# Perceiver layer on one core: last but one cross chunk written out, closing steps moved forward, weight slots exchanged

## What is computed

```python
x = x + cross_attention(layernorm(x), ctx, key_bias, key_mask)   # 16 heads of 32
x = x + self_attention(layernorm(x))     # q, k, v, scores, probabilities, output clamped to [1e-7, 1 - 1e-7]
x = x + experts(layernorm(x))            # 8 experts, each takes its top 32 rows of 128 of every batch:
                                         # gelu(xin @ w1[e]) @ w2[e], 512 -> 2048 -> 512, scattered back
```

## Time and profile before

| | |
|---|---|
| median of 3 runs | 496.81 us (496.67 to 500.01) |
| the profiled execution | 499.95 us, of it span 498.2 us |
| PE busy | 439.1 us (88%) |
| DVE busy | 377.1 us (76%) |
| ACT busy | 288.4 us (58%) |
| POOL busy | 85.6 us (17%) |
| mean granted clock of PE | 0.955 |

### The profile page before, as it was taken

The page is one execution under the profiler, slowest core; times in us unless marked ns, Lnnn a source line. Parts: engine busy times, 40 slices in busy tenths (PEclk is TensorE's granted clock), DMA queues, the critical chain, the costliest instruction groups (busy, mean ns, idle before and its releaser), DMA issues. The chain is left out here.

```text
span 498.2 us, 9477 instructions
## 1 busy us (share of the span) xinstructions
PE 439.1 (88%) x3262; PEld 361.4 (73%) x3262; DVE 377.1 (76%) x495; ACT 288.4 (58%) x594; POOL 85.6 (17%) x87
## 2 busy tenths in 40 slices
PE   0798999999996489997897399999999999999993
PEld 0687888888885377886775378787878787878782
DVE  4679766777777857655697779989898989898963
ACT  0445666666664331356514068787878787878752
POOL 4000000000003201000004214040404040404000
PEclk9999999999999589998998599999999999999998
DMA  6980000000000192231000019999998989898102
GB/s 222 319 313 22 23 23 21 21 21 21 21 21 0 35 349 81 86 108 62 3 2 0 1 52 391 387 387 387 378 374 308 369 305 359 309 369 302 42 0 84
DMA packets 42908, 81.95 MB, mean 164 GB/s; under 512 B 2952, under 2 KB 3080, under 8 KB 42888
## 3 DMA queue, kind: packets, MB, share of 16 engines
q1 hardware_dynamic: 39576, 76.16, 42.8%
q10 hardware_dynamic: 3312, 5.52, 3.2%
HBM read 80.58 MB, written 1.10 MB: 164 GB/s over the span
## 5 line engine op out<-in xcount | busy, mean ns | idle before, releaser
L1010 DVE TENSOR_TENSOR w_lo<-att_w,w_hi 128x2048 fp32r<-128x2048 f32 x60 | 137.8, 2306 | 22.7 <-ACT w_hi L573 22.7
L573 ACT CAST w_hi<-att_w 128x2048 fp32r<-128x2048 f32 x60 | 115.1, 1918 | 15.4 <-PE po L1345 15.4
L422 ACT ACTIVATE big_a<-ps,negm 128x128 f32<-128x128 f32 x176 | 62.2, 402 | 30.1 <-DVE negm L746 30.1
L1345 PE MATMUL po<-w_hi,ht_hi 128*128 128x512 f32 x128 | 51.9, 406 | 0.0
L1345 PE MATMUL po<-w_hi,ht_lo 128*128 128x512 f32 x128 | 50.6, 395 | 0.0
L1345 PE MATMUL po<-w_lo,ht_hi 128*128 128x512 f32 x128 | 50.6, 395 | 0.0
L1055 PE MATMUL pk<-ctx_s,att_w 128*128 128x128 f32 x352 | 42.2, 279 | 0.6 <-DMA ctx_s<-in_ctx_t 0.6
L422 ACT ACTIVATION_READ_ACCUMULATOR big_a<-ps,negm 128x1 f32 x176 | 42.7, 243 | 0.0
L1055 PEld LDWEIGHTS pk<-ctx_s,att_w 128*128 128x128 f32 x352 | 40.1, 192 | 2.9 <-issue 1.8
L743 DVE TENSOR_REDUCE mc<-ps 128x8 f32<-128x1024 f32 x22 | 26.8, 1220 | 13.2 <-PE ps L1122 13.2
L1345 PEld LDWEIGHTS po<-w_hi,ht_lo 128*128 128x128 f32 x128 | 24.1, 188 | 5.7
(11 more groups left out here) (274 smaller groups left out, 980.1 us busy)
## 6 DMA issues: line engine op xcount, KB each, us to landing
att_w<-in_w SPq DMA_DIRECT2D x64, 1024.0 KB, 6.8
ctx_s<-in_ctx_t SPq DMA_DIRECT2D x11, 256.0 KB, 2.5
x_s<-in_x SPq DMA_DIRECT2D x1, 1024.0 KB, 5.8
att_w<-in_wk SPq DMA_DIRECT2D x1, 1024.0 KB, 8.3
att_w<-in_wq SPq DMA_DIRECT2D x1, 1024.0 KB, 10.7
att_w<-in_wv SPq DMA_DIRECT2D x1, 1024.0 KB, 6.9
att_w<-in_wo ACTq DMA_DIRECT2D x1, 1024.0 KB, 6.6
att_w<-in_sq ACTq DMA_DIRECT2D x1, 1024.0 KB, 10.2
```

The costliest lines, as they stand in the source:

```text
L422: ins = a.activation(big_a[:, h], ps[:, c, g * P:(g + 1) * P], ACT.Exp, bias=negm[:, h:h + 1], accum_out=sums[:, h:h + 1])
L573: a.copy(w_hi[:, i % SLOTS], att_w[:, i]).then_inc(hi_ok, 1)
L1010: v.tensor_tensor(w_lo[:, i % SLOTS], att_w[:, i], w_hi[:, i % SLOTS], ALU.subtract).then_inc(lo_ok, 1)
L1345: ins = mm(dst, l, r, start=start and i == 0, stop=i == len(terms) - 1, skip_group_check=True)
```

## The change

The loops over chunks end one earlier, at `prev` = `last` - 1, read from a further entry of `table`, and chunk `prev` is written out with some steps added (`at_end`): DVE forms `reciprocals(0, 2)`, `attended(0)` and `attended(1)` between its copies, PE turns batch 0 between the transposes of the probabilities and the last quarter of the values projection, and ACT and DVE split it. In the last softmax PE issues the out-projections of batches 0 and 1 ahead of and between the transposes of the probabilities; batch 2 is closed between DVE's copies, batch 3 at the end. `maxima` is cut into two halves, and the values' evacuation of the last chunk stands between them. The order of the self attention's turned batches and value projections is changed: `cross_project(3)` ahead of `values_project(0)`, and each `values_project(b)` directly behind `turn_batch(2, b)`. The value weights now go to slot 3 in the prologue; the query weights go to slot 1, split by ACT and DVE in the last softmax and behind it. POOL's two split operations and its `zero` tensor are gone. The self attention's output weights go to slot 1 instead of 3, and the first expert's slots are split in the order 2, 0, 3, 1, with the waits (2, 4, 4, 4).

```diff
-        ot_s = att_w[:, 4, 0].rearrange("p (k t) -> p k t", k=KC)
+        ot_s = att_w[:, 6, 0].rearrange("p (k t) -> p k t", k=KC)
...
-        SPLITS = ((wq_s, 2, in_wq), (wv_s, 1, in_wv), (sq_s, 3, in_sq), (wo_s, 2, in_wo), (sv_s, 1, in_sv), (sk_s, 0, in_sk), (so_s, 3, in_so))
-        TURN_BANKS = [[0, 1, 2, 3], [4, 5, 6, 7], [0, 1, 2, 6], [4] * 4, [4] * 4]
+        SPLITS = ((wq_s, 2, in_wq), (wv_s, 1, in_wv), (sv_s, 3, in_sv), (wo_s, 2, in_wo), (sq_s, 1, in_sq), (sk_s, 0, in_sk), (so_s, 1, in_so))
+        TURN_BANKS = [[0, 1, 2, 3], [4, 4, 0, 7], [5, 4, 1, 2], [4] * 4, [4] * 4]
         V2_BANKS = [3, 0, 1, 4]
-        CROSS_BANKS = [4, 5, 4, 5]
+        CROSS_BANKS = [5, 4, 1, 2]
...
# SP: loads of the first expert's tiles
                 if i == 4:
-                    sp.wait_ge(bt_mm, last + 1)
+                    sp.wait_ge(att_lo_ok, 5)
                 if i == 5:
                     sp.wait_ge(att_lo_ok, 6)
                 if i == 6:
+                    sp.wait_ge(bt_mm, last + 1)
+                if i == 7:
                     sp.wait_ge(att_lo_ok, 7)
...
# POOL
-            g.tensor_tensor(w_hi[:, 1], sv_s, zero[:].unsqueeze(2).broadcast_to([P, KC, D]), ALU.add).then_inc(att_hi_ok, 1)
-            pool.wait_ge(att_hi_ok, 5)
-            g.tensor_tensor(w_lo[:, 1], sv_s, w_hi[:, 1], ALU.subtract).then_inc(att_lo_ok, 1)
...
# ACT
-            with act.Fori(1, last) as t:
+            with act.Fori(1, prev) as t:
                 split_chunk(t + 1)
                 softmax_chunk(t, True)
+            split_chunk(last)
+            softmax_chunk(prev, True)
+            transposed(1, 0)
+            turned_out(last)
             exponents(last, 0)
+            transposed(1, 1)
             exponents(last, 1)
-            turned_out(last)
             rescaling(last)
-            for b in range(B - 1):
-                transposed(1, b)
             exponents(last, 2)
             exponents(last, 3)
+            split_att(4)
             turned_last(last)
+            transposed(1, 2)
             turned_out(last + 1)
-            transposed(2, 0)
             transposed(1, 3)
-            for b in range(1, B):
+            for b in range(B):
                 transposed(2, b)
-            act.wait_ge(att_lo_ok, 5)
             split_att(5)
...
# DVE, end of chunk(t, before, at_end)
                 rescale(t, running(state, t))
-                for c in range(3):
-                    turned_probs(t, c)
+                turned_probs(t, 0)
+                if at_end:
+                    dve.wait_ge(total_ok, t)
+                    dve.wait_ge(summed, t)
+                    reciprocals(0, 2)
+                turned_probs(t, 1)
+                if at_end:
+                    attended(0)
+                turned_probs(t, 2)
                 add_sums(t)
+                if at_end:
+                    attended(1)
+                    transposed(1, 0)
...
# DVE, the last chunk, as it stands after the change
            maximum(last, nm, 0)
            dve.wait_ge(pv_mm, last)
            v_evacuate(last)
            maximum(last, nm, 1)
            moved_maxima(last, nm)
            transposed(1, 1)
            turned_probs(last, 0)
            add_values(prev, last)
            turned_probs(last, 1)
            dve.wait_ge(total_ok, last)
            dve.wait_ge(summed, last)
            reciprocals(2, 3)
            attended(2)
            turned_probs(last, 2)
            rescale(last, running(state, last))
            add_sums(last)
            cross_output(0)
            transposed(1, 2)
            add_values(last, last + 1)
            dve.wait_ge(total_ok, last + 1)
            dve.wait_ge(summed, last + 1)
            reciprocals(3, 4)
            attended(3)
            normed_batch(2, 0)
            transposed(1, 3)
            cross_output(1)
            transposed(2, 0)
            normed_batch(2, 1)
            cross_output(2)
            normed_batch(2, 2)
            transposed(2, 1)
            split_att(4)
            cross_output(3)
            transposed(2, 2)
            normed_batch(2, 3)
...
# PE, chunk(t, before, at_end)
                 turn_probs(t, 3)
+                if at_end:
+                    pe.wait_ge(k_out, t + 2)
+                    turn_batch(1, 0)
                 v_project(t + 1, 3)
                 scores(t + 1)
                 values(t)
...
# PE, behind the loop, as it stands after the change
            chunk(prev, True, at_end=True)
            pe.wait_ge(tr_lo_ok[1], 1)
            turn_batch(1, 1)
            turn_values(last)
            pe.wait_ge(v_out, last + 1)
            pe.wait_ge(att_lo_ok, 4)
            cross_project(0)
            turn_probs(last, 0)
            turn_probs(last, 1)
            cross_project(1)
            turn_probs(last, 2)
            turn_probs(last, 3)
            pe.wait_ge(pt_dve, last * 3 + 1)
            turn_batch(1, 2)
            values(last)
            turn_values(last + 1)
            cross_project(2)
            turn_batch(1, 3)
            turn_batch(2, 0)
            cross_project(3)
            values_project(0)
            turn_batch(2, 1)
            values_project(1)
            turn_batch(2, 2)
            values_project(2)
            turn_batch(2, 3)
            pe.wait_ge(tr_lo_ok[2], B)
            pe.wait_ge(att_lo_ok, 5)
            project_t(1, banks[4:8], q2_mm)
...
-                pe.wait_ge(lo_ok, (2, 3, 3, 4)[q] if isinstance(e, int) and e == 0 else e * 8 + (q + 1))
+                pe.wait_ge(lo_ok, (2, 4, 4, 4)[q] if isinstance(e, int) and e == 0 else e * 8 + (q + 1))
```

More of the change, by code:

```diff
@@ L670, in _ @@
             v.tensor_copy(table[:, 0:n_at], pv[0:1, 0:n_at]).then_inc(table_ok, 1)
-            v.tensor_scalar(table[:, n_at:n_at + 1], pv[0:1, n_at:n_at + 1], -1.0, None, ALU.add).then_inc(table_ok, 1)
+            for i in range(2):
+                v.tensor_scalar(table[:, n_at + i:n_at + i + 1], pv[0:1, n_at:n_at + 1], -1.0 - i, None, ALU.add).then_inc(table_ok, 1)
             statistics(3)
@@ L780, in add_sums, with reciprocals, attended, chunk @@
                 v.tensor_tensor(row, row, sums[:], ALU.add).then_inc(total_ok, 1)
-            def chunk(t, before):
+            def reciprocals(first, end):
+                now = slice(first, end)
+                link(v.tensor_scalar(norm_c[:, now], neg_max[:, now], 0.1 * MASKED, None, ALU.is_lt))
+                link(v.tensor_tensor(total[:, now], norm_c[:, now], total[:, now], ALU.mult))
+                link(v.reciprocal(total[:, now], total[:, now]))
+                link(v.tensor_tensor(norm_c[:, now], norm_c[:, now], total[:, now], ALU.mult))
+            def attended(b):
+                v.tensor_tensor(natural(norm[:, b]), natural(state[:, b]), by_head(norm_c[:, b]), ALU.mult).then_inc(normed[1], 1)
+            def chunk(t, before, at_end=False):
                 nm = running(neg_max, t)
-                maxima(t, nm)
+                maximum(t, nm, 0)
+                maximum(t, nm, 1)
                 if before is not None:
@@ L793, in chunk @@
                 rescale(t, running(state, t))
[L794 to L795 removed]
+                turned_probs(t, 0)
[7 more added lines that the diff above has]
+                turned_probs(t, 2)
                 add_sums(t)
+                if at_end:
+                    attended(1)
+                    transposed(1, 0)
             chunk(0, None)
[L799 removed]
+            with dve.Fori(1, prev) as t:
                 chunk(t, t - 1)
[L802 to L811 removed]
+            chunk(prev, prev - 1, at_end=True)
             def cross_output(b):
@@ L821, in _ @@
             nm = running(neg_max, last)
-            maxima(last, nm)
+            maximum(last, nm, 0)
+            dve.wait_ge(pv_mm, last)
+            v_evacuate(last)
+            maximum(last, nm, 1)
             moved_maxima(last, nm)
-            add_values(last - 1, last)
+            transposed(1, 1)
+            turned_probs(last, 0)
+            add_values(prev, last)
+            turned_probs(last, 1)
             dve.wait_ge(total_ok, last)
             dve.wait_ge(summed, last)
-            reciprocals(0, B - 1)
-            for b in range(B - 1):
-                attended(b)
-            dve.wait_ge(pv_mm, last)
-            v_evacuate(last)
-            transposed(1, 0)
-            transposed(1, 1)
-            transposed(1, 2)
-            rescale(last, running(state, last))
-            turned_probs(last, 0)
-            turned_probs(last, 1)
-            cross_output(0)
-            turned_probs(last, 2)
-            normed_batch(2, 0)
-            cross_output(1)
-            add_sums(last)
+            reciprocals(2, 3)
+            attended(2)
+            turned_probs(last, 2)
+            rescale(last, running(state, last))
+            add_sums(last)
+            cross_output(0)
+            transposed(1, 2)
             add_values(last, last + 1)
@@ L845, in _ @@
             dve.wait_ge(summed, last + 1)
-            reciprocals(B - 1, B)
```

(6 more changed lines are left out.)

85 lines of the change are left out of this document (36 added, 49 removed).

## The result

| | median, us | runs | ratio to before |
|---|---|---|---|
| before | 498.14 (496.51 to 500.01) | 13 | |
| after | 495.03 (493.81 to 496.86) | 13 | 0.9934 [0.9919, 0.9949] |

The kernel is 3.1 us faster, where 5.9 was forecast. Its time of 495.03 us lies inside the stated range (487.5 to 495.5), near its upper end, and 4.1 above the forecast of 490.9. The profiled execution of after took 494.46 us for a span of 492.8; that of before took 499.95 for 498.2, so this pair of traces differs by 5.4 and the medians by 3.1.

A forecast was written before the change was run, and what follows sets the result against it. PE bounds the experts; ahead of them, `negm` held beside POOL's operations delays the last softmax. Query projection 7.6 us earlier, less 1.7 in the first expert, gives 5.9: 496.81 to 490.9 us, range 487.5 to 495.5.

The forecast's parts named there:

- The removed stalls: Last softmax: both `negm` fall from 2.45 and 3.31 us to 0.15; `values(last)` some 10.5 behind `values(prev)`, instead of 26.2.
- the stall at `turn_batch(1, 0)`: Written-out chunk: PE stalls 1.0 us for `attended(0)`, plus 0.4 for the turn; `values(prev)` 1.5 us later.
- the three rounds: Before the query projection: three times turn, 2.0 us round with nothing beside it, then product; PE idles 1.6 each.
- the new wait in the first expert: `hidden(0, 1)` waits for slot 1's split, the fourth: PE stands 1.7 us, paid in full.
- ACT's split: Last softmax: ACT's `split_att(4)`, 1.92 us, beside PE's second out-projection costs nothing; uncovered, up to 1.9.
- D: Rival: engines run dry of instructions in the written-out chunk, up to 3.31 us a stall, 504.1 with four; chance 0.06.
- C: Rival: longer rounds, from `table` reads showing in full or an uncovered split, about +2.7 us, 493.6; chance 0.12.
- A: Rival: clock falls at 168 to 172 us, or before's median runs lose nothing at 172.64: +2.0, 492.9; chance 0.20.
- the last widening: Range 488.4 to 494.6 extended by 0.9 on either side, because the runs of before spread over 3.3 us.
- B: Rival: the low-clock stretch behind 230 us may not come once moved by 7.6 us: 2.0 gained, 488.9; chance 0.12.
- the 2.0 for the clock in Part 2: Last softmax: 2.0 us gained because the first out-projection, 4.90 us at half clock, would run at full clock.
- Part 5: Prologue: one more small DVE instruction and `table` read, and an exchanged load order, cost 0 (bound 0.5 for the reads).

The follow-up runs named there:

- e5: Before with chunk `prev` written out behind the loop, no step moved, slots and POOL's operations kept: 498.49 us, ratio 1.0005.
- e8: The kernel before run once more without an edit, for a second profile: 497.44 us, span 495.7.
- e1: The kernel after run once more without an edit: 495.58 us, ratio to before 0.9938.
- e12: The kernel after, unedited, in one job with its partner that keeps the tile `zero`: 495.03 us, ratio to before 0.9908.
- e9: After with the unused 4-byte tile `zero` allocated again: 492.99 us, ratio to before 0.9903.
- e13: After with the tile `zero` kept, in one job with unedited after: 494.02 us, ratio to before 0.9894.
- e4: After with each `values_project(b)` one turn later and DVE's `split_att(4)` behind the last normalisation: 490.54 us, ratio to before 0.9837.
- e3: After with the self attention's output weights in slot 2, so `hidden(0, 1)` waits for the second split: 493.54 us, ratio to before 0.9893.
- e6: After with PE's `turn_batch(1, 0)` behind the last quarter of `v_project` in the written-out chunk: 494.38 us, ratio to before 0.9919.
- e10: After with the edits of e3, e4 and e6 together and the tile `zero` kept: 487.45 us, ratio to before 0.9791.

## Why the prediction was right and wrong

**The mechanism of every part was right.** The removed stalls, the stall at `turn_batch(1, 0)`, the three rounds and the new wait in the first expert stand in the trace where they were put, with 1.7 for 1.5, 10.7 for 10.5, 25.7 for 25.9, and 1.7 to 1.8 for 1.7. ACT's split was covered: it ends at 169.08, and `turned_last` starts 0.20 behind it on PE's release. D has no support (e5), and C none either: PE's one idle for issue in the tail is 0.28. Of A the first half didn't happen: the clock is 1.00 from 150 to 200 us in after. Its second half, that the median runs of before may lose nothing of the 2.0 at 172.64, pointed the right way.

That the time lies inside the stated range is in part luck. Its ends before the last widening, 488.4 and 494.6, lie 0.5 and 1.0 outside B's 488.9 and C's 493.6, and no reason is given for that; from B's and C's own figures the range would have ended at 494.5. Faster by over 1%, which had a chance of 0.58, didn't come: it was 0.7%.

**What failed is the step from one execution to the medians.** The sum was made on the profiled execution, and "its difference carried to the median". The forecast lies 4.1 us too low, and this has two parts.

The first is the base. The median of before was 496.81 over three runs and is 498.14 over thirteen: 1.3 us, whatever the change does.

The second is the size, 5.9 where the medians show 3.1, and here the mis-sized term is the 2.0 for the clock in Part 2. The first out-projection took 4.90 us in the profile that the sum was made on, 3.78 in e8 and 4.61 in e5, which has the same order; after takes 2.90. So the term is 0.9, 1.7 or 2.0, depending on the execution. The table sets all three profiles of the old order beside the three of after (after, e1, e12):

| stretch | before, e8, e5 | after, e1, e12 | difference of the means | forecast |
|---|---|---|---|---|
| start to `values(0)` | 52.36, 52.09, 52.91 | 53.10, 52.89, 53.89 | +0.84 | 0 |
| `values(0)` to `values(prev)` | 104.4 to 104.5 | 106.1 to 106.2 | +1.70 | +1.5 |
| `values(prev)` to `values(last)` | 26.20, 25.06, 25.88 | 10.71 in each | -15.00 | -15.7 |
| `values(last)` to query projection | 19.3 in each | 25.7 in each | +6.44 | +6.6 |
| query projection to `hidden(0, 0)` | 87.94, 86.44, 87.79 | 86.18, 87.52, 86.19 | -0.76 | 0 |
| `hidden(0, 0)` to `hidden(0, 2)` | 6.0 to 6.1 | 7.9 in each | +1.81 | +1.7 |
| `hidden(0, 2)` to the end | 201.95, 202.34, 201.95 | 203.04, 203.06, 203.07 | +0.98 | 0 |
| sum | | | -4.0 | -5.9 |

The three jobs with after in them measured -3.1, -3.2 and -4.4. Up to 1 us of the first two is not assigned; each median is uncertain by about as much. Rival B was right that the stretch behind 230 us might be missing after the change, but took it for a gain of the change; it was missing from a profile of before as well, and present in e1. It is worth 1.3 to 1.5 us, where B had 2.0.

The Trainium skill (TensorE: Matmul & The Clock Gate, "The HAM clock gate (the "warmup" mystery)") says that the same kernel shows different numbers of slow products at its start from one run to the next. The traces of this case show such a difference in mid kernel too: 87.5 us with a fall and 86.2 without, for the same kernel over the same products.

**A term was missing: the stretch from `hidden(0, 2)` to the end was put at zero and cost 1.0 us.** The removed tile `zero` was costed at nothing; that other tiles stand behind it in SBUF was not thought of. Each expert took 0.08 us more, 0.6 in all. The rest is in the last scatter, whose first four products took 0.52 us in before and 0.81 in after:

```profile
491.65 0.52 PE L1385 MATMUL ps<-y_hi,back_now 32*128 32x512 f32 x4 [2.25 <-DVE y_lo L1034]
```

```profile
485.71 0.81 PE L1398 MATMUL ps<-y_hi,back_now 32*128 32x512 f32 x4 [2.25 <-DVE y_lo L1045]
```

This is the clock again: it is granted at 1.00 in before from 491 to 493 us and at 0.50 in after from 486 to 487. In every profile it falls to 0.50 some 3.5 to 7.4 us ahead of the end. In before it falls 3.7 ahead, behind these products, and from the last expert's last product to the end it takes 9.2 us; in after, e1 and e12 it falls 7.0 to 7.2 ahead, at these products or before them, and the same way takes 9.7. e8 has 9.7 as well, and e9 and e13 have 9.2, so the execution or the timing decides, and whether the change itself brings it isn't shown.

Whether the prologue costs something (Part 5) isn't shown either. `values(0)` starts between 52.0 and 53.9 us over all seventeen profiles; the eleven with the added read of `table` have a mean of 53.0, the six without it 52.7.

**Where the gain went.** `values(last)` comes 12.7 to 13.8 us earlier, counted from `values(0)` against the two profiles of before. Of this the change gives 6.4 back at once, by an order in which each product waits for its own turn (4.2 of it recovered in e4), and 1.7 in the first expert (recovered in e3). The gains of e3, e4, e6 (by its trace) and of the tile add up to 2.0+5.0+0.5+1.0 = 8.5 us below after; e10 measured 7.6 below, in another job. More than half of what the best kernel gains over before is thus not in the change itself but in taking back its side effects.

## What to carry to other kernels

Where a clock or a state varies from run to run, take two profiles before making a sum on one, and ask of each slow stretch that the change is to remove whether a typical run has it. A turn, its split and its product in series want another batch's product between them: an order that puts each product directly behind its own turn cost 4 us here. And removing a tile, however small, moves all tiles behind it; keep its place until the pace of the long loops has been compared.

## What the runs showed of the hardware

- A tile of one float per partition, used by nothing, made the split products of the experts 0.3% faster: 36 products in 8.37 to 8.39 us with it, 8.42 to 8.44 without, over all profiles.
- Both `negm` (128x8 elements) took 2.45 and 3.31 us beside POOL's elementwise operations of 128x2048, and 0.17 in every trace without them. Each ended 0.03 us behind POOL's instruction, so the small one of DVE stood until that was done. The reductions of 128x1024 out of PSUM just ahead of them, 1.23 and 1.21 us, took the same beside POOL as without it.
- For the same kernel the granted clock fell to 0.50 in one execution (e1, at 224 us) and stayed at 1.00 in another (after), with PE busy for 6.06 and 6.25 of the 8 us before. The fall is worth 1.3 to 1.5 us.
- Where the clock falls at the end of the kernel decides 0.5 us: 9.7 us from the last expert's last product to the end in the profiles where it falls some 7 us ahead of the end, 9.2 in those where it falls 3.5 to 5.8 ahead.
